# Separate orders for start, loop and end of a decoder layer on one core, with another order of the first loads and other PSUM banks

## What is computed

```python
x = _layernorm(x + attn(x, Wq, bq, Wk, bk, Wv, bv, Wo, bo, orf))
#   q, k, v = split(x @ W.T + b);  phi(y) = (exp(y @ orf.T / d**.25 - |y|^2 / (2 sqrt d)) + EPS) / sqrt(m)
#   kv = einsum(phi(k), v);  out = (phi(q) @ kv) / (phi(q) . sum(phi(k)));  out @ Wo.T + bo
x = _layernorm(x + xattn(ctx_1024, x, ctx_1024, Wk, Wq, Wv))   # k and v from ctx, per head 16 x 16
#   softmax(q @ k.T / sqrt(16)) @ v
x = _layernorm(x + ffn(x, w_gate, w_up, w_down))
#   bitlinear(y, w) = act_quant(y) @ weight_quant(w).T;  down(silu(gate(x)) * up(x))
#   weight_quant: scale = 1 / mean |w|;  clip(round(w * scale), -1, 1) / scale
```

## Time and profile before

| | us |
|---|---|
| median of 3 runs | 505.86 (505.42 to 506.31) |
| the profiled execution | 507.6 |
| its span, first to last instruction | 505.9 |
| mean granted TensorE clock, share of full speed | 0.972 |

### The profile page before, as it was taken

The page is one execution under the profiler, slowest core; times in us unless marked ns, Lnnn a source line. Parts: engine busy times, 40 slices in busy tenths (PEclk is TensorE's granted clock), DMA queues, the critical chain, the costliest instruction groups (busy, mean ns, idle before and its releaser), DMA issues.

```text
span 505.9 us, 18665 instructions
## 1 busy us (share of the span) xinstructions
PE 437.2 (86%) x6566; PEld 304.7 (60%) x6566; DVE 450.7 (89%) x1355; ACT 429.1 (85%) x908; POOL 365.0 (72%) x789
## 2 busy tenths in 40 slices
PE   4568888889899999999999999999999988866541
PEld 2235666666677667677767776777777766543220
DVE  4667786889999999999999999999999998999771
ACT  2247788979999999999999999999999998866632
POOL 1447766768888888888888888888888876754332
PEclk9979899999999999999999999999999999999975
DMA  7666556776666666666666666666666777532212
GB/s 180 235 127 110 121 125 116 110 136 94 137 136 140 137 142 138 139 140 145 145 145 145 145 135 141 136 138 143 137 140 130 136 137 138 76 74 53 54 42 62
DMA packets 192644, 64.07 MB, mean 127 GB/s; under 512 B 172384, under 2 KB 192352, under 8 KB 192608
## 3 DMA queue, kind: packets, MB, share of 16 engines
q1 hardware_dynamic: 190080, 60.46, 58.2%
q10 hardware_dynamic: 2528, 3.15, 1.7%
HBM read 17.31 MB, written 4.19 MB: 43 GB/s over the span
## 4 chain that ended last, share of the span: by engine, by line
PE 56%; ACT 15%; DMA 11%; DVE 7%; issue 5%; POOL 3%; SPq 1%; ACTq 0%; POOLq 0%; DVEq 0%
PE bank L1129 11%; PE bank L1333 8%; PE bank L1360 4%; PE bank L1304 3%; PE bank L1181 3%; PE bank L1223 3%; DMA tT<-pkT 3%; DMA ffn_ld<-in_L_ffn_w_down_dram 3%; ACT pT L629 3%; PE bank L1143 3%; ACT pT L628 2%; DMA tT<-nmT 2%; PE bank L1238 2%; PE bank L1320 2%; ACT x L556 2%
## 5 line engine op out<-in xcount | busy, mean ns | idle before, releaser
L1129 PE MATMUL bank<-wq_hi,xT 128*128 128x512 f16 (+1 forms) x256 | 72.1, 337 | 4.0 <-DVE vv L814 2.6
L432 POOL TENSOR_TENSOR ve<-mv,lneps 128x1 f32<-128x1 f32 x96 | 19.2, 200 | 67.8 <-DVE mv L864 52.7
L436 POOL TENSOR_TENSOR rs<-ve,mhalf 128x1 f32<-128x1 f32 x96 | 54.7, 569 | 0.0
L628 ACT ACTIVATE pT<-bank 128x512 f32<-128x512 f32 x64 | 37.9, 592 | 12.6 <-PE bank L1294 10.6
L944 DVE SCALAR_TENSOR_TENSOR g<-th,bank 128x512 f32<-128x512 f32 x64 | 42.9, 671 | 3.9 <-ACT th L651 3.7
L556 ACT ACTIVATE x<-y,nmr,rs 128x256 f32<-128x256 f32 x64 | 39.8, 621 | 7.4 <-DVE y L1005 3.8
L895 DVE TENSOR_REDUCE negm<-bank 128x4 f16<-128x512 f32 x64 | 43.5, 679 | 2.8 <-PE bank L1258 2.7
L896 DVE TENSOR_REDUCE negm<-bank 128x4 f16<-128x512 f32 x64 | 43.6, 681 | 0.0
L1360 PE MATMUL bank<-downT,hqT 128*128 128x256 bf16 x256 | 34.3, 279 | 10.3 <-DMA hqT<-hq 10.3
L575 ACT ACTIVATE phk<-bank 128x512 f32<-128x512 f32 x64 | 39.3, 616 | 4.6 <-PE bank L1148 4.6
L1129 PE MATMUL bank<-wq_lo,xT 128*128 128x256 f16 (+1 forms) x128 | 43.0, 336 | 0.0
(11 more groups left out here) (184 smaller groups left out, 1574.7 us busy)
## 6 DMA issues: line engine op xcount, KB each, us to landing
xs<-in_x_dram SPq DMA_DIRECT2D x32, 128.0 KB, 2.2
cs<-in_ctx_dram SPq DMA_DIRECT2D x32, 128.0 KB, 2.2
xr<-in_x_dram SPq DMA_DIRECT2D x32, 128.0 KB, 2.2
out_dram<-ot SPq DMA_DIRECT2D x32, 128.0 KB, 1.8
ffn_ld<-in_L_ffn_w_gate_dram ACTq DMA_DIRECT2D x1, 1024.0 KB, 8.7
ffn_ld<-in_L_ffn_w_up_dram ACTq DMA_DIRECT2D x1, 1024.0 KB, 11.5
ffn_ld<-in_L_ffn_w_down_dram ACTq DMA_DIRECT2D x1, 1024.0 KB, 13.7
pkAT<-pkA SPq DMA_TRANSPOSE x64, 3.2
```

Source lines behind the costliest of these rows:

```text
L436: g.tensor_tensor(rs[n - 1][:, :], ve[n - 1][:, :], mhalf[:, :], ALU.pow).then_inc(done[f"pw{n}"], 1)
L628: sc.activation(pT[:, grp, 0, :, :], even.rearrange("p (c t) -> p c t", c=4), ACT.Exp, scale=0.25)
L1129: last = T.matmul(o, xT[:, 2 * part + c, :], w[:, c, cols], start=(n == 0), stop=(n == 5))
```

## The change

The steps stay the same. Each engine now has three lists: `ramp(i)` with `lead`, `iteration(i, par)` and `drain(i)` with `trail`. The unrolled start and end no longer follow the loop's order and have lags of their own; `ramp` starts at -15 to -88, as an engine's steps need. The lags of POOL, ACT, DVE and PE between steps of one tile stay nearly as they were, apart from the rotation of the lists.

- **Loads.** SP loads x of tiles 0 and 1 around the projection weights, then the biases, Wo, `bob`, then `w_gate`. `w_down` and `w_up` follow behind x of tile 3, for which SP waits on `xlo` of tile 1. All are on SP's queue now. POOL no longer waits for `bob` ahead of everything.
- **Once-only work.** `scales_of`, `rounds_of` and `clips_of` all stand between the qk read-outs of tiles 1 and 5 (before: of tiles 2 and 6), the copies of the transposed matrices up to one iteration earlier. The memsets of DVE come first.
- **Banks.** 18 of the 34 places of steps in PSUM move; the waits for them change, and PE's are written per tile in the unrolled parts (`only_at`) and once for the loop (`wait_looped`).
- **Waits.** Some waits are spelled out that were implied before (`s1` for `m1`, `hq0` for `hqT_`, `kT` for `hi`).

```diff
-        at_g0 = pb[3][:, :]
-        at_u1 = pb[5][:, :]
-        at_st0a = pb[2][:, :]
-        at_phk1 = pb[7][:, :]
-        at_s1b = pb[6][:, :]
+        at_g0 = pb[2][:, :]
+        at_u1 = pb[0][:, :]
+        at_st0a = pb[3][:, :]
+        at_phk1 = pb[0][:, :]
+        at_s1b = pb[0][:, :]
         at_mT = pb[0][:, 0:64]
-        at_st1b = pb[7][:, :]
+        at_st1b = pb[1][:, :]
...
-        at_aT = pb[7][:, 0:256]
-        at_dn = pb[1][:, 0:256]
+        at_aT = pb[1][:, 0:256]
+        at_dn = pb[5][:, 0:256]
...
+        def wait_looped(eng, name, t, off=0):
+
+            if looping(t):
+                eng.wait_ge(done[name], t + off + 1)
+
+        def only_at(eng, t, tile, name, producer_tile):
+
+            if isinstance(t, int) and t == tile:
+                eng.wait_ge(done[name], producer_tile + 1)
+
+        def lead(step, i, lag, until):
+
+            t = i - lag
+            if 0 <= t < until:
+                step(t, t % 2)
+
+        def trail(step, i, lag, since):
+
+            t = i - lag
+            if since <= t < TILES:
+                step(t, t % 2)
...
-        def run(eng, iteration, lags, first):
-
-            for i in range(first):
-                iteration(i, i % 2)
-            with eng.Fori(first, TILES - 1, 2) as i:
+        def run(eng, ramp, iteration, drain, ramps, first, last, drains):
+
+            for i in range(*ramps):
+                ramp(i)
+            iteration(first - 2, 0)
+            iteration(first - 1, 1)
+            with eng.Fori(first, last - 1, 2) as i:
                 iteration(i, 0)
                 iteration(i + 1, 1)
-            for i in range(TILES, TILES + lags):
-                iteration(i, i % 2)
+            for i in range(*drains):
+                drain(i)
...
+            def load_first(t):
+                sp.dma_start(xs[:, t, :], x[t]).then_inc(moved["x"][t], 16)
+
+            load_first(0)
             for n, w in enumerate((Wq, Wk, Wv)):
                 sp.dma_start(wld[:, n, :, :], w.rearrange("(o p) i -> p o i", p=P)).then_inc(w_in[n], 16)
...
+            load_first(1)
...
             def load_x(t, par):
                 wait(sp, "xlo", t, -2)
+                if isinstance(t, int) and t < 2:
+                    return
                 sp.dma_start(xs[:, par, :], x[t]).then_inc(moved["x"][par], 16)
...
                 pool.wait_ge(zeroed, 11)
-                pool.wait_ge(bo_in, 16)
...
-            load_ffn()
-            load_down()
-            evacuate_wo()
...
+                once(magnitudes[0], i, -11)
+                once(feature_weights, i, -15)
...
+                once(magnitudes[1], i, -9)
...
             def st1(t, par):
-                first_time(pe, t, 0, ffn_out, 4)
-                first_time(pe, t, 1, ffn_out, 5)
...
+                wait_looped(pe, "aT", t, 2)
+                wait_looped(pe, "gl1", t, -2)
                 wait_moved(pe, "row", t, par)
-                wait(pe, "aT", t, 2)
-                wait(pe, "gl1", t, -2)
```

More of the change, by code:

```diff
@@ L496, in _, with ramp @@
-            run(pool, iteration, 11, 12)
+            def ramp(i):
+                lead(hq0, i, -16, 6)
+                lead(hq1, i, -16, 6)
+                lead(ya2, i, -18, 8)
+                once(late_packs, i, -39)
+                lead(xlo, i, -25, 14)
+                lead(chi, i, -21, 10)
+                once(late_constants, i, -52)
+                lead(phe, i, -22, 11)
+                lead(clo, i, -21, 10)
+                lead(rs2, i, -18, 7)
+                lead(nf, i, -24, 13)
+                lead(xb_, i, -22, 12)
+                lead(rs3, i, -15, 4)
+                lead(xhi, i, -26, 14)
+                lead(rs1, i, -21, 10)
+                lead(lo, i, -24, 13)
+                lead(xqf, i, -18, 7)
@@ L499, in _ @@
+            run(pool, ramp, iteration, drain, (-52, -10), 16, 30, (-9, 4))
         @block.scalar
@@ L1067, in _ @@
+            run(dve, ramp, iteration, drain, (-15, 3), 14, 30, (17, 28))
         @block.tensor
```

897 lines of the change are left out of this document (665 added, 232 removed), and 6 rows, old and new, of the table done.

## The result

The changed kernel takes 508.39 us in the median of seven runs (507.63 to 512.36), the kernel before 505.86 in seven (502.2 to 507.18) on the same chip. The ratio is 1.0065 with a 95% interval of 1.0034 to 1.0097: a small loss, but one that is clear of the noise. The prediction was 498.7 us, 488 to 507.

What follows compares the result with a forecast made beforehand. The prediction took DVE, ACT and PE, all full in the loop, as the bound. Its terms, -1.5 - 5.3 + 1.6 - 2.0 = -7.2 us, taken from the median of 505.9, gave 498.7 us, range 488 to 507.

Steps and rivals of the forecast that it cites:

- What bounds the kernel: From 150 to 404 us DVE, ACT and PE are full; a new order can win only outside, at most 1.8 us inside.
- Start, -1.5 us: Loads at the start: `w_up` lands near 24.5 us, means come near 27.3 instead of 28.75; 4 us won to 3 lost.
- rival 2: Start: the one load queue is the limit, `w_up` lands near 29 us, 3 us lost; total 503.2 us, chance 0.08.
- the first transpose of x comes at about 12.3 us: Start: PE's and ACT's lists keep Wo ahead of tile 0's x, so its first transpose comes just after Wo's.
- 2 us: Start: what the first transpose of x, behind Wo at about 12.3 us, would win alone.
- Ramp, -5.3 us: Read-outs of tiles 0 to 10: better order wins 5.3 us, bounds 0 and 12.
- the 12 named: Ramp, tiles 0 to 10: less than 12 us should remain in which no engine is full.
- `y1` ahead of `rd`: DVE's ramp list: moving `y1` forward wins about 0.6 us in each of some three stretches.
- A third of the ceiling: Ramp: order alone can win at most 16.1 us; a third of that, 5.3 us, was taken.
- Loop, +1.6 us, bounds -1 to +6: Tiles 10 to 31: lists nearly the old ones, 0.08 us lost per tile over 20 tiles; 1 us won to 6 lost.
- Rival 3, the row transfer: Loop: row transfer delays `st1` and the period, up to 0.7 us per tile, 14 us; total 511 us, chance 0.12.
- Drain, -2.0 us: After the loop: 0.5 us from an earlier `ad3`, 1.5 from DVE's idle time; 5 us won to 1 lost.

Runs made afterwards that it cites:

- experiment 1: Changed kernel with `qnt` and `nlo` ahead of `at` and `sg` in DVE's loop: 502.26 us, ratio 0.9942.
- experiment 6: Kernel of experiment 5 with DVE's `nlo` also moved behind `sg` and `bs3`, directly ahead of `m0`: 520.47 us, ratio 1.0311.
- experiment 2: Changed kernel with `nlo` alone ahead of `at` and `sg` in DVE's loop, `qnt` where it was: 509.1 us, ratio 1.0075.
- experiment 3: Changed kernel with DVE's 18 loop iterations written out instead of a hardware loop: 504.13 us, ratio 0.9980.
- experiment 4: Changed kernel with POOL's `lo` behind `xqf` in its loop, as in the kernel before: 512.37 us, ratio 1.0146.
- experiment 7: Changed kernel with the edits of experiment 1 and experiment 3 together: 500.59 us, ratio 0.9924.
- experiment 8: Kernel of experiment 1 with `rd` and `hc` again ahead of `y1` in DVE's ramp list: 501.67 us.
- experiment 9: Kernel of experiment 7 with DVE's whole ramp list in its loop's order: 500.47 us, ratio 0.9922.
- experiment 10: Kernel of experiment 7 with `aT`, the copy into `attT`, ahead of `thi` in ACT's loop: 500.8 us.
- experiment 5: Kernel before the change with `lo` ahead of `xqf` in POOL's loop: 514.15 us, ratio 1.0173.

## Why the prediction was wrong, step by step

**What bounds the kernel.** Right. In the loop three engines are full, and a stall of DVE goes into the time nearly whole in the changed kernel (experiment 1), to two thirds in experiment 6.

**Start, -1.5 us.** The means were forecast for 27.3 us and came at 25.9 in the first profile and at 27.4 to 27.8 in the next four: right, with the first one early because its first `nlo` was not held and `w_gate` landed at 15.4 instead of 16.2 to 16.5 us. That the queue is not the limit was right too: `w_down` took 5.0 us and `w_up` 7.4 us from issue to landing, so that `w_up` was there at 23.5 us; rival 2 falls. The transposes of tile 0 behind it on the queue were issued at 22.1 and had landed by 26.7 us, and the gain at the means was there all the same. But the read-out of tile 0 came at 17.6 us once and at 18.4 to 18.7 in the four profiles of experiments 1 to 4, against 18.6 before. The step "the first transpose of x comes at about 12.3 us" named the right place, though it came at 13.3, behind Wo. The "2 us" named there, which the sum doesn't use, were not to be had: DVE's first sum, which begins when `w_gate` has landed, stood ahead of the read-out as well. The 1.5 us of the sum are a gain at the means; at the read-out of tile 0, where the table divides, they don't appear.

**Ramp, -5.3 us.** The size was right: -7.8 in the first profile, -5.1 to -6.7 in experiments 1 to 4, 7 and 8, which share these lists up to one move. Part of the spread goes with the clock. Between the read-outs of tiles 0 and 10 PE's granted clock is at half for 10.2 us before and for 3.4 in the changed kernel; in experiments 2 and 3 it is at half for the same 10.2 us as before, and the ramp is still 5.2 and 5.5 us shorter. Taken stretch by stretch as for the earlier trace rows, the busiest engines of the changed kernel add up to 95.8 of 103.2 us: 7.4 us with no engine full, under the 12 named. The last row of the ramp, answering, has PE full:

```profile
107.70:120.80 13.10, 13.06 (x206) 9.29 (x204) 12.88 (x43) 12.56 (x29) 11.16 (x25) 1.00 0.69 118
```

The reasons were wrong. `y1` ahead of `rd` was to bring 1.8 us and brings none that the runs can tell, and DVE's whole ramp order brings none (experiments 8 and 9). A third of the ceiling, taken with these reasons, gave the right size by luck.

**Loop, +1.6 us, bounds -1 to +6.** This is the step that failed: +10.0. The sum took the moves within DVE's and POOL's lists at nothing, and they cost eight held `nlo` and a held `xm`, 7.6 us by experiment 1. "Here the lists are nearly the old ones" was true, and the swap of `lo` and `xqf` on POOL was in the lists that I compared. I asked of each move only who waits on a semaphore for whom. I never asked what DVE and POOL run at the same moment, though the trace of before had the sign of it. One `nlo` of 32 took 0.93 us, while a `lo` ran that itself took 1.67 (it began beside the rounding at 39.11 us of the earlier trace rows):

```profile
39.67 1.67 POOL L423 TENSOR_TENSOR pkA<-qk,pkA 128x512 f16<-128x512 f32 x1 [2.00 <-ACT pkA L518]
...
40.58 0.93 DVE L833 TENSOR_TENSOR pkA<-nrm,pkA 128x32 f16<-128x32 f32 x1
```

The upper bound of 6 us came from the row transfer and excluded the rest. Without the stall (experiments 1 and 7) the loop costs +1.5 and +0.5 us, inside the bounds, but not by the cycle through `attT` (experiment 10).

**Rival 3, the row transfer, slower, 511 us.** It came nearest to the time, by a mechanism that is not there. Between 200 and 390 us `st1` (L1674) waits in the changed kernel like this:

```profile
PEld bank L1674 <- ACT attT L612: 3.0, 7, 0.4
...
PE bank L1674 <- DMA tT<-nmT: 1.2, 7, 0.2
```

0.2 us at the longest. The chance of 0.12 for slower was spent on this one place; the class "two engines that exclude each other" had none. That it named about the right time was luck.

**Drain, -2.0 us.** Measured -0.8. The row that answers the earlier trace rows:

```profile
483.45 0.60 ACT L651 ACTIVATE x<-y,nmr,rs 128x256 f32<-128x256 f32 x1 [2.96 <-DVE y L1153]
```

It starts 78.2 us behind the read-out of tile 31 instead of 79.5, so 1.3 us are won up to here, and 0.6 are lost from here to the end. That is less than the lists win in other profiles, and the difference goes with the clock. In the earlier trace rows PE's granted clock is 1.00 up to 484 us. In the changed kernel it falls to half for a while at about 475 us (columns as above):

```profile
473.00:476.00 3.00, 1.99 (x34) 1.10 (x34) 2.11 (x12) 2.52 (x6) 0.85 (x2) 0.75 0.00 0
476.00:479.00 3.00, 2.61 (x9) 1.35 (x9) 0.81 (x4) 1.82 (x4) 1.40 (x3) 0.50 0.00 0
```

some 70 us behind the read-out of tile 31. In the kernel of experiment 7, with the same drain lists, it holds until 475 us, 77 us behind it:

```profile
469.00:472.00 3.00, 1.67 (x7) 0.70 (x8) 2.25 (x7) 1.85 (x4) 1.32 (x2) 1.00 0.48 51
472.00:475.00 3.00, 1.05 (x8) 0.70 (x8) 2.96 (x7) 0.32 (x1) 1.95 (x8) 1.00 0.31 83
```

There the drain takes 99.8 us, 2.1 less than before, as forecast; in experiment 1, where the clock falls to 0.50 at 458 and again at 469 us, it takes 101.9. The twelve profiles with these drain lists fall into three groups by the time at half clock in the 80 us behind the read-out of tile 31: 1.9 us of it and a drain of 99.8 and 99.9 us (two), 5.0 to 7.4 and 100.2 to 101.1 (seven), 10.6 to 10.9 and 101.7 to 102.2 (three). With the old lists it is 0.1 us and 101.9 before, and 10.2 and 102.9 in experiment 5. The term was a property of the lists and of the clock, and I had counted the lists alone. That the clock's fall causes the 2 us is read from these profiles and was not tried apart.

**The sum.** -1.0 - 7.8 + 10.0 - 0.8 is +0.4 us of span. Against the median the changed kernel looks 2 us worse, since the execution profiled before was 1.7 us above its median and the one after was at its own.
